# Order of the score matmuls within a group: both halves of a maxima unit first, then the two exponential score matmuls

## The reference

```
x = x + cross_attention(layernorm(x), context)   # 16 heads of width 8, softmax over 512 + 256 keys
x = x + experts(layernorm(x))                    # 8 experts, the best 2 for each token
```

## Time and profile before

| | |
|---|---|
| three runs, median (lowest to highest) | 559.42 us (555.78 to 559.89) |
| the profiled execution, its own time | 551.65 us |
| its span in the trace | 550.1 us |
| TensorE matmuls, busy | 463.2 us (84%) |
| VectorE, busy | 355.2 us (65%) |
| ScalarE, busy | 290.5 us (53%) |
| GpSimd, busy | 181.5 us (33%) |
| mean granted TensorE clock | 0.919 |

### The profile page before, as it was taken

One profiled execution on the slowest core, in us unless ns is written; L12 is line 12 of the kernel. 1 busy time (PEld: TensorE's weight loads), 2 busy tenths in 40 slices (PEclk: granted clock), 3 DMA queues, 4 the chain that ended last, 5 costly groups with the idle time before them and its releaser, 6 DMA issues. The chain is left out here.

```text
span 550.1 us, 10607 instructions
## 1 busy us (share of the span) xinstructions
PE 463.2 (84%) x3467; PEld 273.7 (50%) x3468; DVE 355.2 (65%) x646; ACT 290.5 (53%) x584; POOL 181.5 (33%) x381
## 2 busy tenths in 40 slices
PE   2489999999999999999999987536499999999940
PEld 1255555554555555555555543435266666666630
DVE  7698797786887887887888850669234333333317
ACT  2237776777777777777777776310033333333310
POOL 6141231412312311412300000104446766676630
PEclk9659999999999999999999999655599999999985
DMA  6512224243243242322212100610111111111126
GB/s 176 126 38 68 65 77 109 75 106 89 77 114 95 78 114 75 94 77 62 53 51 62 38 3 0 193 37 0 19 25 41 43 43 35 43 38 38 43 69 181
DMA packets 32254, 38.10 MB, mean 69 GB/s; under 512 B 5604, under 2 KB 20580, under 8 KB 32212
## 3 DMA queue, kind: packets, MB, share of 16 engines
q1 hardware_dynamic: 27252, 30.79, 20.8%
q0 software_dynamic: 2560, 5.25, 3.7%
q10 hardware_dynamic: 2400, 1.51, 1.1%
HBM read 16.58 MB, written 4.72 MB: 39 GB/s over the span
## 5 line engine op out<-in xcount | busy, mean ns | idle before, releaser
L464 DVE TENSOR_REDUCE max_part<-max_ps 128x2 f32<-128x1024 f32 (+1 forms) x192 | 227.2, 1221 | 55.3 <-PE max_ps L562 42.1
L423 ACT ACTIVATE probs<-ring_ps 128x512 f32<-128x512 f32 x384 | 199.7, 602 | 69.8 <-PE ring_ps L585 68.0
L585 PE MATMUL ring_ps<-blocks,keys 64*128 64x512 f32 x384 | 144.9, 461 | 2.9 <-ACT probs L423 2.6
L595 PE MATMUL pv_ps<-probs,value_cols 128*32 128x256 f32 x1536 | 102.6, 385 | 0.0
L562 PE MATMUL max_ps<-keys,blocks 64*128 64x512 f32 x256 | 85.8, 455 | 8.6 <-DMA blocks<-masked 6.6
L1019 DVE TENSOR_TENSOR hidden<-up_ps,silu 128x512 f32<-128x512 f32 x40 | 27.7, 692 | 82.0 <-PE up_ps L1109 79.8
L585 PEld LDWEIGHTS ring_ps<-blocks,keys 64*128 64x128 f32 x384 | 64.8, 186 | 31.6 <-ACT probs L423 28.4
L339 POOL CAST maxes<-rowmax 128x8 fp32r<-128x8 f32 x32 | 6.3, 198 | 173.0 <-DVE rowmax L471 173.0
L912 ACT ACTIVATE hiddenT<-at_ps 128x512 f32<-128x512 f32 x40 | 23.9, 597 | 74.7 <-PE at_ps L1126 66.2
L595 PEld LDWEIGHTS pv_ps<-probs,value_cols 128*32 128x32 f32 x1536 | 40.2, 109 | 36.6 <-issue 10.9
L562 PEld LDWEIGHTS max_ps<-keys,blocks 64*128 64x128 f32 x256 | 41.4, 195 | 33.9 <-issue 22.4
(11 more groups left out here) (148 smaller groups left out, 459.0 us busy)
## 6 DMA issues: line engine op xcount, KB each, us to landing
keys<-parts SPq DMA_DIRECT2D x96, 96.0 KB
blocks<-masked SPq DMA_DIRECT2D x93, 64.0 KB
ctx_v_sb<-ctx_v_dram SPq DMA_DIRECT2D x8, 256.0 KB, 2.9
gate<-gateT_dram SPq DMA_DIRECT2D x8, 256.0 KB, 2.7
up<-upT_dram SPq DMA_DIRECT2D x8, 256.0 KB, 2.7
y_in<-pick_outs SPq DMA_DIRECT2D x8, 256.0 KB, 4.9
raw<-ctx_kT_dram SPq DMA_DIRECT2D x7, 256.0 KB, 2.7
h_rows<-h SPq DMA_DIRECT2D x4, 256.0 KB, 4.9
```

What stands on the lines that cost most here:

```text
L423: act.activation(probs[par][:, k, PAIR * a:PAIR * (a + 1)], bank("exp", s * XUNITS + u)[:].rearrange("p (g n) -> p g n", n=N), ACT.Exp).th ...
L464: vec.reduce_max(out, bank, axis=AX.X).then_inc(max_done, 1)
L585: pe.matmul(ps[:], keys[rows, t, k * P:(k + 1) * P], blocks[rows, t], start=True, stop=True)\
L595: mm = pe.matmul(pv_ps[ROWS * g:ROWS * (g + 1), 0:N], value_cols[:, t, k, g, :], probs[q % 2][:, k, g, :], start=(k == 0), stop=(k == KT - 1))
```

## The change

Within each group, the loop over the two row tiles is split in two. Before, each turn of the loop issued one maxima half (row tile 1, then 0) and one exponential score matmul (row tile 0, then 1). Now both maxima halves are issued, and then both exponential score matmuls. No instruction, operand, semaphore or wait is added or removed; each instruction takes its own wait along. The order in a pair of groups becomes m1, m0, e0, e1, m1', m0', e2, e3.

```diff
@@ -638,10 +638,11 @@
                             project_keys_queries(b + 2)
                     if i == 2 and has_scores(s + 1):
                         transpose_maxima(s + 1)
-                    for a in range(2):
-                        if has_scores(s + 2):
+                    if has_scores(s + 2):
+                        for a in range(2):
                             max_half(s + 2, i, 1 - a)
-                        if has_scores(s):
+                    if has_scores(s):
+                        for a in range(2):
                             exp_unit(s, 2 * i + a)
                     if i == 3 and 1 <= s <= QUADS:
                         transpose_out(s - 1)
```

## The result

| | before | after |
|---|---|---|
| median of the runs | 557.84 us (4 runs, 555.78 to 559.89) | 576.66 us (4 runs, 572.75 to 577.74) |
| profiled execution, span | 550.1 us | 576.2 us |
| TensorE matmuls, busy | 463.2 us | 474.7 us |
| VectorE, busy | 355.2 us | 355.0 us |
| ScalarE, busy | 290.5 us | 290.4 us |

What follows compares the result with a forecast made beforehand. Bound: the latency loop e0, ScalarE, e3, no full engine. 81 pairs x 0.23 = +18.6 us, less 1.6 us for earlier transposes, gave +17.0 on 559.42: 576.4 us, range 564 to 587.

Steps and rivals of the forecast that it cites:

- e3: Last exponential score matmul of a pair, needing e0's bank; forecast to start at t0 + 1.48 us instead of 1.25.
- The bound: Each pair of groups: latency loop from e0 over ScalarE to e3 sets its length; maxima matmuls are hidden under it.
- 0.23 us a pair: e0, one place later on row tile 0, ends 0.23 us later; paid in 81 pairs, +18.6 us.
- e2 in r = 2: Six pairs (0, 1) with the key and query projection: e2's 0.23 us delay is paid there as well.
- m0' in r = 1: Seven pairs (0, 1): m0' one place earlier ends VectorE's L520 sooner, so transposes go 0.23 us earlier, gaining 1.6 us.
- The sign that was off: TensorE's waits for ScalarE at L585: their sum was to go up from 21.7 us by some 16 us.
- VectorE as the bound: VectorE ends last, so earlier maxima halves shorten 81 pairs by 0.23 us: 541 us on the median; chance 0.05.
- Absorbed: e0's start or end barely moves, so only the 1.6 us gain remains: 558 us on the median; chance 0.08.
- Program order across tiles: Pairs (4, 5): m0 waits for m1's second matmul, e0 ends 0.53 us later: 586 us on the median; chance 0.12.
- a delay of 0.34: All pairs: e0 delayed by the distance of the starts, +25.9 us, 585; covered by a rival of chance 0.12.

Runs made afterwards that it cites:

- experiment 5: The changed kernel run again, unchanged, against the kernel before: 574.48 us, ratio 1.0321.
- experiment 1: Against the kernel before, the new order in the first group of each pair only: 577.73 us, ratio 1.0361.
- experiment 8: First exponential of each pair cut to 256 columns, with a small fill: in the kernel before 543.98 us, ratio 0.9744; in the changed kernel 560.36 us, ratio 1.0033.
- 10: Against the kernel before, each step passed in four phases of three exponential score matmuls instead of three of four: 543.05 us, ratio 0.9746.
- 11: Four phases of three exponential score matmuls with the studied maxima-first order, against the kernel before: 537.49 us, ratio 0.9612.
- experiment 2: Against the kernel before, the new order in the second group of each pair only: 557.86 us, ratio 1.0016.
- experiment 4: Against the kernel before, program order of e1 and m0 swapped (m1, e0, e1, m0), order on each row tile kept: 558.52 us, ratio 1.0022.
- 9: The kernel before run again, unchanged, for a second trace: 557.76 us, ratio 1.0001.

## Why the prediction was right

The forecast was +17.0 us and 576.4; the ratios are worth +18.1 us (0.0325 x 557.84) and, in experiment 5, +17.9, with a median of 576.66 and 574.48. That the median came within 0.3 us is luck: the forecast stood on 559.42, which is 1.6 us above the median of the four runs before, and its difference is 1.1 us short. The steady part is the better test: from the copy of step 3 to that of step 29 the forecast has 26 x 0.69 - 7 x 0.46 = 14.7 us, and the traces have 264.48 - 250.05 = 14.4.

- **The bound.** A closed loop from e0 over ScalarE to e3, with the maxima hidden under it. Shown two ways: e0's place is paid with e3's start in full (experiment 1), and a shorter exponential is gained in full in the plain pairs and undoes the change (8). With a ring that suffices for each phase the price is gone as well (10, 11), though there more was moved at once.
- **0.23 us a pair.** Measured from e3's start: 1.48 for 1.25. The steps give 0.67 or 0.68 for three pairs, so 0.225 each; experiment 2 shows that e2's part is nothing in a plain pair.
- **e2 in r = 2.** +0.68 there after the change, and +0.22 from e2 alone in experiment 2: right.
- **m0' in r = 1.** The step grew by 0.23 (2 x 0.23 - 0.23), right to the hundredth; the reason given, that both reductions start earlier, holds. What I did not see is how easily it turns: what stands ahead of m0' made the same step 0.17 longer than its sum in experiment 1, and 0.25 longer than before in experiment 4.
- **The sign that was off.** TensorE's waits for ScalarE at L585 were to grow by some 16 us and grew by 25. The prediction took e3's delay for the whole of it; the load ahead of e3's moved too. This changes no time.
- **Rivals.** VectorE as the bound: refused, by experiment 8 as well. Absorbed: refused. Program order across tiles: refused in the pairs (4, 5), where the after trace has e3 at t0 + 1.43 (for 1.19 before), not 0.53 later, and by experiment 4; a delay of 0.34 is refused by the steps.
- **What was left out.** The falls of the clock, about 1.3 us in the changed kernel's two traces each, would close most of the difference between 17 and 18; the executions without a trace don't show whether they had one. The 26 us between the two first profiled spans were more than the order's effect: 14.4 in the steps 4 to 29, 0.46 in the last interval, 5.3 behind it, and 5.9 ahead of them, in the first steps, where the lower clock lasted longer (16 product matmuls took 1.93 us at 42.09 in the changed kernel, and 1.07 at 41.46 before). The last two are chance in so far as a second trace of each kernel shows other values (experiments 5 and 9).

## What to carry to other kernels

Look for two engines that wait for each other once per round. In such a loop the latency from the first producer over the consumer to the producer that waits for its buffer can set the length of the round, though no engine is full. Here what moved the first producer (0.23 us a pair) or the consumer's release (0.22) was paid or gained in full. Work that needs no such buffer belonged between the two ends of the loop: ahead of its first producer it cost 0.23 a pair, behind its last one up to as much. Where a round asked for no more buffers than the ring has, the better order turned: the instruction that may be held went last and the free work ahead of it, for 5.6 us.

## What the runs showed of the hardware

- The order of a matmul within its row tile is what sets its start, as long as nothing ahead of it in the program is held: swapping the program order of two on different tiles changed no plain step (8.71 for 8.72 us), while swapping two on the same tile moved the end of each by 0.23 us. A matmul behind one that is held waits with it, also on the other tile: m0' behind e3 started at t0 + 1.26 for t0 + 0.80 (experiment 4).
- TensorE's matmuls were modelled as busy for 257 of 268 us and yet nearly each pair waited on ScalarE (70 waits in 268 us). The wait ahead of e3 shows as no idle time in the matmul row before and as 0.29 us after; its weight load had 0.72 us after, and ScalarE's own idle time (1.04 and 1.27) shows the loop best.
- Slightly less dense work on TensorE (pairs longer by 0.2 us of waiting) came with falls of the granted clock from 1.00 to 0.50 in the middle of the steady stretch, one or two in each of four traces, each 1.2 to 1.4 us. The other ten traces have none: two of the kernel before, those of the experiments 2 and 4, the four with a shorter exponential, and the two four-phase kernels.
